# Last stage of a two-layer gated kernel: biases in a freed contraction row, transpositions between the halves of the up-projection, statistics and scaled products interleaved

## The chip, the cores and the metric

The kernel runs on one core of one Trainium2 chip, as one program from the first load to the last store. The metric is the device time of one execution in microseconds (us). The engines are PE (TensorE; PEld is its weight load), DVE (VectorE), ACT (ScalarE), POOL (GpSimd) and SP (SyncE, which issues the transfers).

## The reference, cut to what matters

Two layers work on x, 64 batches of 128 tokens by 256 values: cross attention and a routed feed-forward network, each scaled by tanh of a gate. Both networks get their input through a plain normalisation (mean taken off, divided by the root of the variance). The change touches the last network alone:

```python
# tail of reference(): xf is the normalised input, E = 4 experts, top 2
gate_scores = xf @ gate_W + gate_b
topk_scores, topk_idx = jax.lax.top_k(gate_scores, K_TOP)
weights = jax.nn.softmax(topk_scores, axis=-1)
def expert(w1, bb1, gg1, bbe1, w2, bb2, gg2, bbe2):
    h = jax.nn.relu(_layernorm(xf @ w1 + bb1, gg1, bbe1))
    return _layernorm(h @ w2 + bb2, gg2, bbe2)
...
exp_out = all_out[topk_idx, jnp.arange(BN)[:, None]]
out = jnp.sum(weights[..., None] * exp_out, axis=1)
return (out + xf).reshape(B, N, D)
```

The kernel adds tanh(gate) times this to its input x3. All four experts are computed for every token, and the weight of an unchosen one is zero.

## The kernel before, in words

There are four stages: attention of layer 0, the experts of layer 0, attention of layer 1, and the last stage, the feed-forward network of layer 1. The last stage goes through 64 batches b = 0..63 of 128 tokens, one step s for each, as a pipeline over several batches: in step s the up-projection works on batch s, the down-projection on s-1, the scaled products on s-2, the final sum on s-3. Steps 16 to 55 run in a loop of 8 steps a turn, the others are written out. Each engine has its own queue, which it works through strictly in the order in which `fstep` writes it; semaphores order the engines against each other. No planner or scheduler moves anything.

One batch goes this way (lines of the profile):

- DVE takes mean and variance of the input (`fst`, L1500, L1504), POOL makes the reciprocal root (`frs`, L645 to L651, four instructions), ACT writes the normalised `xf` (L824).
- PE transposes `xf` (L1151), ACT and DVE split it into a high and a low part (`xft_hi` L829, `xft_lo` L1490).
- PE: up-projection (L1117, L1120) in two halves of two experts each, into banks 2 and 3 of `ps`. Each half is one matmul for the bias (`ones2` by `b12`) and six for 2 blocks x (high.high, high.low, low.high), all 512 columns wide. The gate scores are six matmuls of 4 columns (L1142).
- DVE takes the statistics of the four experts (`h_st`, four instructions, then `h_mv`, four, L1423 and L1430), POOL makes scale and shift from them (`h_rs`, L670 to L676), ACT writes the normalised `z1` (L837, four), PE transposes it (L1184, eight), ACT applies scale, shift and relu (`a_t`, L857, eight).
- PE: down-projection (L1162 bias, L1165 eight matmuls, which the trace counts as sixteen) into banks 6 and 7. DVE takes statistics (`k_st`, `k_mv`), POOL makes `k_rs`, the weight times the reciprocal root `k_rw`, and mean times that (L631 to L638); DVE forms the scaled products `u2g` (L1454, four), POOL sums them (`u2s` L663, `u2t` L680), adds x3 (`rest` L682) and then the `mixed` part (L689).
- The weights of the chosen experts: DVE picks them (L1477 to L1486), ACT takes the exponential, DVE builds them (L1440 to L1447), POOL adds the two (L657), PE turns them (L1175), and one matmul adds shifts and means (L1130).

Three rules of the code matter below. `up1` of a batch waits until all four `z1` of the batch before are written (`z_act`). `u2g` waits until all four instructions of `k_rstd` are done. `h_rs` waits for all four `h_mv`.

Of the kernel before, what the change touches and what calls it, by code (L numbers as in the profile page):

```python
# [5 lines left out]
P = 128  # L6
# [118 lines left out]
def flamingo_gated(nc, x, ctx_in, consts, gates, wq, wk, wv, wp, b_proj, router, w1_0, b1_0, w2_0, b2_0,  # L125
                   gate_w, gate_b, w1_1, b12_1, g1_1, be1_1, w2_1, g2_1, be2_1, out):
# [25 lines left out]
    with es:  # L152
# [174 lines left out]
        gw_hi = psb("gw_hi", [P, C, E1], F32R)  # L327
        gw_lo = psb("gw_lo", [P, C, E1], F32R)
        gb_in = psb("gb_in", [P, E1])
        b12_in = psb("b12_in", [2, 2, E1, D])  # L330
        b12_hi = psb("b12_hi", [2, 2, E1, D], F32R)
        b12_lo = psb("b12_lo", [2, 2, E1, D])
        b12 = psb("b12", [P, 2, E1, D], F32R)
# [18 lines left out]
        def signals(prefix, arrivals, counts):  # L352
# [32 lines left out]
            dict(st=2, rstd=4, xf_done=1, x_turned=1, x_hi_done=1, x_lo_done=1, gates_done=1, gates_read=1, gate_steps=4,  # L385
# [31 lines left out]
        def _(sp):  # L417
# [20 lines left out]
            def layer1_weights():  # L438
                sp.wait_ge(s_padded, 3)
                for dst, src in ((w1f, w1_1), (w2f, w2_1), (gw_in, gate_w), (gb_in, gate_b), (b12_in, b12_1), (g1_in, g1_1),  # L440
                                 (be1_in, be1_1), (g2_in, g2_1), (be2_in, be2_1)):
                    sp.dma_start(dst[0:E1] if dst is be2_in else dst[:], src).then_inc(s_fw, 16)
                sp.dma_start(be2_in[E1:2 * E1], g2_1[0]).then_inc(s_fw, 16)
# [96 lines left out]
        def _(pool):  # L540
# [83 lines left out]
            def fstep(s):  # L624
# [14 lines left out]
                b = s + 1  # L639
                if b.within(B):  # L640
                    st = f["rstd"]
                    pool.wait_ge(f["st"].of(b), f["st"].at(b))
                    if (b - 1).begun:
                        pool.wait_ge(f["xf_done"].of(b - 1), f["xf_done"].at(b - 1))
                    nc.gpsimd.tensor_tensor(frs[:, 0:1], fmv[:, 1:2], eps, ALU.add).then_inc(st.sem, 1)  # L645
                    pool.wait_ge(st.of(b), st.at(b, 1))
                    nc.gpsimd.tensor_tensor(frs[:, 1:2], frs[:, 0:1], neg_half, ALU.pow).then_inc(st.sem, 1)
                    pool.wait_ge(st.of(b), st.at(b, 2))
                    nc.gpsimd.tensor_tensor(frs[:, 2:3], fmv[:, 0:1], frs[:, 1:2], ALU.mult).then_inc(st.sem, 1)
                    pool.wait_ge(st.of(b), st.at(b, 3))  # L650
                    nc.gpsimd.tensor_tensor(frs[:, 3:4], frs[:, 2:3], neg_one, ALU.mult).then_inc(st.sem, 1)  # L651
# [6 lines left out]
                b = s - 2  # L658
                if b.within(B):
                    pool.wait_ge(f["u_done"].of(b), f["u_done"].at(b))  # L660
                    if (b - 1).begun:
                        pool.wait_ge(f["summed"].of(b - 1), f["summed"].at(b - 1))
                    nc.gpsimd.tensor_tensor(u2s[:], u2g[:, 0:2, :], u2g[:, 2:4, :], ALU.add).then_inc(f["halved"].sem, 1)  # L663
# [14 lines left out]
                if b.within(B):  # L678
                    pool.wait_ge(f["halved"].of(b), f["halved"].at(b))
                    nc.gpsimd.tensor_tensor(u2t[:], u2s[:, 0, :], u2s[:, 1, :], ALU.add).then_inc(f["summed"].sem, 1)  # L680
                    pool.wait_ge(f["summed"].of(b), f["summed"].at(b, 1))
                    nc.gpsimd.tensor_tensor(rest[:, b.parity, :], u2t[:], x3[:, b.off % 8, :], ALU.add).then_inc(f["summed"].sem, 1)  # L682
                b = s - 3
                if b.within(B):
# [4 lines left out]
                    nc.gpsimd.tensor_tensor(x4[:, b.parity, :], rest[:, b.parity, :], mixed[:, b.parity, :], ALU.add).then_inc(f["mix"].sem, 1)  # L689

            pool.wait_ge(s_fset2, 10)
# [4 lines left out]
        def _(act):  # L696
# [113 lines left out]
            act.wait_ge(s_fw, 16 * 10)  # L810
            nc.scalar.activation(w1_hi[:], w1f[:], ACT.Copy).then_inc(s_fset, 1)
            nc.scalar.activation(gw_hi[:], gw_in[:], ACT.Copy).then_inc(s_fset, 1)
            nc.scalar.activation(b12_hi[:], b12_in[:], ACT.Copy).then_inc(s_fset, 1)
            nc.scalar.activation(be2_in[0:2 * E1], be2_in[0:2 * E1], ACT.Copy, scale=g_t[0:2 * E1, 3:4]).then_inc(s_fset, 1)
            act.wait_ge(s_fset, 4)
            act.wait_ge(s_fset2, 10)

            def fstep(s):
                b = s + 1
                if b.within(B):  # L820
                    act.wait_ge(f["rstd"].of(b), f["rstd"].at(b))
                    if (b - 8).begun:
                        act.wait_ge(f["mixed_done"].of(b - 8), f["mixed_done"].at(b - 8))
                    nc.scalar.activation(xf[:, b.off % 8, :], x3[:, b.off % 8, :], ACT.Identity, scale=frs[:, 1:2], bias=frs[:, 3:4])\  # L824
                        .then_inc(f["xf_done"].sem, 1)
                    act.wait_ge(f["x_turned"].of(b), f["x_turned"].at(b))
# [22 lines left out]
                b = s  # L849
                if b.within(B):  # L850
                    if (b - 2).begun:
                        act.wait_ge(f["down1_done"].of(b - 2), f["down1_done"].at(b - 2))
                    for e in range(E1):
                        if e % 2 == 0:
                            act.wait_ge(f["z_turned"].of(b), f["z_turned"].at(b, e // 2 + 1))
                        for c in range(C):
                            nc.scalar.activation(a_t[:, b.parity, e, c, :], ps[:, 4 + e // 2, (e % 2 * 2 + c) * P:(e % 2 * 2 + c + 1) * P],  # L857
                                                 ACT.Relu, scale=g1_in[:, e, c:c + 1], bias=be1_in[:, e, c:c + 1])\
                                .then_inc(f["a_done"].sem, 1)
# [5 lines left out]
        def _(pe):  # L865
# [240 lines left out]
            pe.wait_ge(s_fset2, 10)  # L1106

            def fstep(s):
                b = s
                if b.within(B):  # L1110
# [3 lines left out]
                    for half in range(2):  # L1114
                        dst = ps[:, 2 + half, :]
                        two = slice(2 * half, 2 * half + 2)
                        pe.matmul(dst, ones2[:], b12[:, 0, two, :].rearrange("p e n -> p (e n)"), start=True, stop=False)  # L1117
                        for c in range(C):
                            for xt, w in ((xft_hi, w1_hi), (xft_hi, w1_lo), (xft_lo, w1_hi)):
                                mm = pe.matmul(dst, xt[:, b.parity, c, :], w[:, c, two, :].rearrange("p e n -> p (e n)"),  # L1120
                                               start=False, stop=(c == C - 1 and xt is xft_lo))
                        mm.then_inc(f["up1_done"].sem, 1)
# [9 lines left out]
                if b.within(B):  # L1132
# [6 lines left out]
                    k = 0  # L1139
                    for c in range(C):  # L1140
                        for xt, w in ((xft_hi, gw_hi), (xft_hi, gw_lo), (xft_lo, gw_hi)):
                            mm = pe.matmul(ps[:, 1, 128:128 + E1], xt[:, b.parity, c, :], w[:, c, :], start=(k == 0), stop=(k == 5))  # L1142
                            k += 1
                    mm.then_inc(f["gates_done"].sem, 1)
                b = s + 1
                if b.within(B):
# [3 lines left out]
                    for c in range(C):  # L1150
                        mm = pe.transpose(ps[:, 0, c * P:(c + 1) * P], xf[:, b.off % 8, c * P:(c + 1) * P], ident)  # L1151
                    mm.then_inc(f["x_turned"].sem, 1)
                b = s - 1
                if b.within(B):
                    if (b - 1).begun:
                        pe.wait_ge(f["u_done"].of(b - 1), f["u_done"].at(b - 1))
                    for e in range(E1):
                        if e % 2 == 0:
                            pe.wait_ge(f["a_done"].of(b), f["a_done"].at(b, 4 * (e // 2) + 4))
                        dst = ps[:, 6 + e // 2, (e % 2) * D:(e % 2 + 1) * D]  # L1160
                        if e % 2 == 0:
                            pe.matmul(ps[:, 6 + e // 2, :], ones2[:], b12[:, 1, e:e + 2, :].rearrange("p e n -> p (e n)"),  # L1162
# [13 lines left out]
                b = s  # L1176
                if b.within(B):
                    if (b - 1).begun:
                        pe.wait_ge(f["a_done"].of(b - 1), f["a_done"].at(b - 1))
                    for e in range(E1):  # L1180
                        if e % 2 == 0:
                            pe.wait_ge(f["z_act"].of(b), f["z_act"].at(b, e + 2))
                        for c in range(C):
                            mm = pe.transpose(ps[:, 4 + e // 2, (e % 2 * 2 + c) * P:(e % 2 * 2 + c + 1) * P],  # L1184
                                              z1[:, b.parity, e, c * P:(c + 1) * P], ident)
                        if e % 2 == 1:
                            mm.then_inc(f["z_turned"].sem, 1)
# [5 lines left out]
        def _(dve):  # L1193
# [12 lines left out]
            for n in range(2):  # L1206
# [140 lines left out]
                if n == 0:  # L1347
# [43 lines left out]
                    nc.vector.memset(b12[:].bitcast(F32), 0.0).then_inc(s_padded, 1)  # L1391
# [4 lines left out]
            dve.wait_ge(s_fw, 16 * 10)  # L1396
# [4 lines left out]
            nc.vector.tensor_tensor(gw_lo[:], gw_in[:], gw_hi[:], ALU.subtract).then_inc(s_fset2, 1)  # L1401
            nc.vector.tensor_tensor(b12_lo[:], b12_in[:], b12_hi[:], ALU.subtract).then_inc(s_fset2, 1)
            dve.wait_ge(s_fset2, 5)

            nc.vector.tensor_scalar(b12_lo[:], b12_lo[:], hilo_mask[:, 1:2], None, ALU.mult).then_inc(s_fset2, 1)
            dve.wait_ge(s_fset2, 6)
            nc.vector.scalar_tensor_tensor(out=b12[0:2].rearrange("p a e n -> p (a e n)"),
# [182 lines left out]
```

## Time and profile before

| | us |
|---|---|
| median of 3 runs (lowest, highest) | 2548.15 (2542.39, 2556.09) |
| the profiled execution's own time | 2547.97 |
| its span in the trace | 2546.2 |
| last stage: first to last up-projection | 1878.38 to 2511.48 |
| PE busy over the span | 2336.5 (92%) |
| DVE, ACT, POOL busy over the span | 1640.8, 1155.4, 1131.4 |

The granted TensorE clock is 0.979 on average. Busy shares are averages over four unlike stages; the rows below are therefore of the last stage alone. A PE row's length is modelled, and matmuls overlap, so the distance from one start to the next is what counts on PE. POOL's lengths are rough as well.

### The profile page before, as it was taken

Reading aid. Unit: us, or ns where it says so; the run is one execution under the profiler, and the core shown is the slowest. Engines: PE = TensorE matmul, PEld = TensorE weight load, DVE = VectorE, ACT = ScalarE, POOL = GpSimd, SP = SyncE. Lnnn points to the kernel's source line nnn. Section 1 sums busy time; section 2 is a strip of 40 time slices with the busy share of each in tenths; the row PEclk is TensorE's granted clock in tenths of the full one; section 3 lists DMA queues with packets and bytes.
Section 4 is the critical chain, followed back from the end, with each engine's and each line's share of the span. In section 5 each row is a group of like instructions: output and inputs, shape, how many; then the busy total and the mean of one; then the engine's idle time right before and its main releaser. Section 6 shows DMA issues by size and latency. Waiting matters only on the chain.

```text
span 2546.2 us, 57620 instructions
## 1 busy us (share of the span) xinstructions
PE 2336.5 (92%) x19280; PEld 1934.2 (76%) x19280; DVE 1640.8 (64%) x4890; ACT 1155.4 (45%) x2327; POOL 1131.4 (44%) x2072
## 2 busy tenths in 40 slices
PE   6998989999699999999799999999969999999997
PEld 4777777777499998999666676676748887878885
DVE  4776767777455565555355555555557877777775
ACT  3444544454233333333244444444436565556563
POOL 3455555555200000000244444444327777777776
PEclk9999999999799999999899999999979999999998
DMA  8111111112221122221111111111200000000000
GB/s 266 46 56 54 56 52 54 56 56 72 96 85 56 64 86 86 71 84 50 58 55 58 58 57 58 54 56 58 76 23 28 26 29 27 25 25 29 25 25 16
DMA packets 125253, 147.10 MB, mean 58 GB/s; under 512 B 13818, under 2 KB 117506, under 8 KB 122754
## 3 DMA queue, kind: packets, MB, share of 16 engines
q1 hardware_dynamic: 118916, 127.80, 15.5%
q0 software_dynamic: 6144, 16.79, 2.1%
q8 instruction: 114, 1.87, 0.3%
q14 instruction: 79, 0.65, 0.1%
HBM read 85.82 MB, written 58.72 MB: 57 GB/s over the span
## 4 chain that ended last, share of the span: by engine, by line
PE 71%; DVE 11%; issue 8%; POOL 4%; ACT 4%; DMA 1%; SPq 1%; POOLq 0%; DVEq 0%; ACTq 0%
PE ps L1098 11%; PE ps L1083 10%; PE ps L924 7%; PE ps L1005 5%; PE ps L1165 5%; PE ps L954 5%; PE ps L885 4%; PE ps L1120 4%; PE ps L900 4%; PE ps L938 3%; PE ps L948 3%; DVE o_n L1233 2%; PE ps L989 2%; PE ps L880 2%; ACT z L837 2%
## 5 line engine op out<-in xcount | busy, mean ns | idle before, releaser
L1216 DVE TENSOR_REDUCE nmax<-ps 128x8 f32<-128x1024 f32 x256 | 311.7, 1223 | 102.6 <-PE ps L900 96.1
L553 POOL TENSOR_TENSOR km_r<-qk,cst 128x512 fp32r<-128x512 f32 x128 | 153.5, 1199 | 407.9 <-ACT qk L733 407.9
L801 ACT ACTIVATE hid<-ps,b_in 128x512 f32<-128x512 f32 x192 | 132.4, 690 | 371.7 <-PE ps L1083 371.7
L709 ACT ACTIVATE prob_t<-ps 128x1024 f32<-128x1024 f32 x256 | 248.1, 1021 | 95.3 <-PE ps L885 95.3
L578 POOL COPY slot_in<-slot_all 128x1 int32 (+1 forms) x64 | 11.4, 178 | 575.9 <-DMA eo_d<-eo 575.9
L1165 PE MATMUL ps<-w2f,a_t 128*128 128x256 f32 x1024 | 243.4, 381 | 0.0
L1098 PE MATMUL ps<-w_hi,hid_hi 128*128 128x256 f32 x768 | 219.1, 285 | 0.0
L1098 PE MATMUL ps<-w_hi,hid_lo 128*128 128x256 f32 x768 | 217.3, 283 | 0.0
L1098 PE MATMUL ps<-w_lo,hid_hi 128*128 128x256 f32 x768 | 217.3, 283 | 0.0
L1165 PEld LDWEIGHTS ps<-w2f,a_t 128*128 128x128 f32 x1024 | 195.5, 191 | 27.3
L733 ACT ACTIVATE qk<-ps 128x512 f32<-128x512 f32 x128 | 76.4, 597 | 282.8 <-PE ps L954 282.8
L837 ACT ACTIVATE z<-ps,h_rs 128x256 f32<-128x256 f32 x256 | 123.5, 563 | 152.5 <-POOL h_rs L676 152.5
L857 ACT ACTIVATE a_t<-ps,be_in,g_in 128x128 f32<-128x128 f32 x512 | 182.7, 447 | 0.8 <-PE ps L1184 0.2
L1222 DVE TENSOR_TENSOR nmax_x<-ps,cst 128x512 fp32r<-128x512 f32 x128 | 88.5, 692 | 140.7 <-PE ps L975 140.7
L1083 PE MATMUL ps<-xgt_hi,w_hi 128*128 128x512 f32 x384 | 150.5, 392 | 3.7 <-issue 2.2
L938 PE MATMUL ps<-w_v,c_t 128*128 128x256 f32 x512 | 148.4, 413 | 3.4 <-DMA c_t<-in_ctx_in_dram 3.4
L1083 PE MATMUL ps<-xgt_lo,w_hi 128*128 128x512 f32 x384 | 150.1, 391 | 0.0
L1083 PE MATMUL ps<-xgt_hi,w_lo 128*128 128x512 f32 x384 | 150.1, 391 | 0.0
L1454 DVE SCALAR_TENSOR_TENSOR u2g<-ps,k_rw,g_in 128x256 f32<-128x256 f32 x256 | 106.2, 478 | 67.8 <-POOL gw L638 67.8
L1386 DVE TENSOR_TENSOR eo<-ps,b_in 128x256 f32<-128x256 f32 x96 | 34.0, 418 | 177.8 <-PE ps L1098 177.8
L1098 PEld LDWEIGHTS ps<-w_lo,hid_hi 128*128 128x128 f32 x768 | 147.4, 192 | 0.0
L1098 PEld LDWEIGHTS ps<-w_hi,hid_hi 128*128 128x128 f32 x768 | 147.2, 192 | 0.0
(190 smaller groups left out, 6278.9 us busy)
## 6 DMA issues: line engine op xcount, KB each, us to landing
c_t<-in_ctx_in_dram SPq DMA_DIRECT2D x128, 128.0 KB, 2.0
x_d<-x SPq DMA_DIRECT2D x128, 128.0 KB
w_raw<-in_w_dram SPq DMA_DIRECT2D x16, 1024.0 KB, 7.7
slots_d<-zeros SPq DMA_DIRECT2D x12, 1024.0 KB, 8.7
xg<-slots_d SPq DMA_DIRECT2D x24, 512.0 KB, 4.7
eo_d<-eo SPq DMA_DIRECT2D x24, 512.0 KB, 3.2
x_in<-in_x_dram SPq DMA_DIRECT2D x64, 128.0 KB, 2.1
x_in<-x_d SPq DMA_DIRECT2D x64, 128.0 KB, 2.1
```

The costliest lines, as they stand in the source:

```text
L553: nc.gpsimd.tensor_tensor(dst, src.unsqueeze(2).to_broadcast([P, 2, 2, P]), head_mask.unsqueeze(1).unsqueeze(3).to_broadcast([P, 2, 2, P]) ...
L709: nc.scalar.activation(prob_t[:, 8 * h:8 * h + 8, :].rearrange("p a k -> p (a k)"), scores[:, 2 * h:2 * h + 2, :].rearrange("p a k -> p (a ...
L801: nc.scalar.activation(hid[:, fc % 2, :], ps[:, 4 + fc % 2, 0:G], ACT.Gelu, bias=b1_in[:, e.parity, fc:fc + 1]).then_inc(z["hid_done"].sem, 1)
L837: nc.scalar.activation(z1[:, b.parity, e, :], ps[:, 2 + e // 2, (e % 2) * D:(e % 2 + 1) * D], ACT.Identity, scale=h_rs[:, 1, e:e + 1], bia ...
L857: nc.scalar.activation(a_t[:, b.parity, e, c, :], ps[:, 4 + e // 2, (e % 2 * 2 + c) * P:(e % 2 * 2 + c + 1) * P], ACT.Relu, scale=g1_in[:, ...
L924: mm = pe.matmul(b5[32 * g:32 * g + 32, j * P:(j + 1) * P], v_aug[:, p, h, :], prob_t[:, r, :], start=True, stop=True, tile_position=(0, 3 ...
L938: mm = pe.matmul(b6[:, 0:D], c_t[:, b.off % 4, c, :], w_v[:, c, :], start=(c == 0), stop=(c == C - 1))
L954: mm = pe.matmul(b5[:, (part + m) * P:(part + m + 1) * P], w[:, c, m * P:(m + 1) * P], src[:, c, :], start=(c == 0), stop=(c == C - 1))
L1083: mm = pe.matmul(ps[:, 4 + fc % 2, 0:G], w[:, q, at:at + P], xt[:, g.parity, c, :], start=(k == 0), stop=(k == 5))
L1098: mm = pe.matmul(ps[:, i, 0:D], hd[:, fc, i * P:(i + 1) * P], w[:, q, at:at + D], start=(fc == 0 and k == 0), stop=(fc == FC - 1 and k == 2))
L1165: mm = pe.matmul(dst, a_t[:, b.parity, e, c, :], w2f[:, e, c, :], start=False, stop=True, skip_group_check=True)
L1216: nc.vector.tensor_reduce(nmax[:, b.parity, 2 * h:2 * h + 2, 0:4], scores[:, 2 * h:2 * h + 2, :].rearrange("p a (r k) -> p a r k", k=P), A ...
```

## The change

1. **Biases.** The normalised input sums to zero over its 256 values. So the first value is minus the sum of the others, its row of the weights can be subtracted from the other 255 rows, and the contraction row that is freed takes the constant 1 and the bias. `xf` gets a 257th column that holds 1, and PE transposes columns 1 to 256. The subtraction (`w1f - w1_first`, `gw_in - gw_first`) is done once on DVE ahead of the stage, from a further 1 MB load. The two bias matmuls of the up-projection and DVE's bias for the gate scores go; the bias of the down-projection stays.
2. **Gate scores.** Four matmuls in place of six: the high part of the input by high and low weights side by side (8 columns), the low part by the high weights (4 columns). DVE adds the two groups of 4 columns with two instructions in place of one.
3. **Order on PE:** first half of up(b), transpositions of z1(b-1), second half of up(b), then the rest as before.
4. **Order on DVE:** statistics of the first half of h(b), two scaled products, statistics of the second half, `h_mv`, the other two scaled products. Before: four scaled products, then the statistics of both halves.
5. **Order on POOL and ACT:** on POOL `h_rs` goes ahead of `u2s`, and `frs` to the end of the step, one batch further ahead. On ACT `a_t` goes one step later, to the place ahead of `xft_hi`.
6. The down-projection waits for two scaled products ahead of each half, where it waited for all four.

```diff
 # PE
+            def up(b, half):
+                two = slice(2 * half, 2 * half + 2)
+                for c in range(C):
+                    for xt, w in ((xft_hi, w1_hi), (xft_hi, w1_lo), (xft_lo, w1_hi)):
+                        mm = pe.matmul(ps[:, 2 + half, :], xt[:, b.parity, c, :], w[:, c, two, :].rearrange("p e n -> p (e n)"),
+                                       start=(c == 0 and w is w1_hi and xt is xft_hi), stop=(c == C - 1 and xt is xft_lo))
+                mm.then_inc(f["up1_done"].sem, 1)
...
-                        pe.matmul(dst, ones2[:], b12[:, 0, two, :].rearrange("p e n -> p (e n)"), start=True, stop=False)
...
+                    for c in range(C):
+                        pe.matmul(ps[:, 1, 128:128 + 2 * E1], xft_hi[:, b.parity, c, :], gw_hl[:, c].rearrange("p h e -> p (h e)"),
+                                  start=(c == 0), stop=False, skip_group_check=True)
+                        mm = pe.matmul(ps[:, 1, 128:128 + E1], xft_lo[:, b.parity, c, :], gw_hl[:, c, 0, :],
+                                       start=False, stop=(c == C - 1), skip_group_check=True)
...
+                            if (b - 1).begun:
+                                pe.wait_ge(f["u_done"].of(b - 1), f["u_done"].at(b - 1, e + 2))
...
 # DVE, ahead of the stage
-            dve.wait_ge(s_fw, 16 * 10)
+            dve.wait_ge(s_fw, 16 * 11)
+            nc.vector.tensor_tensor(w1f[:], w1f[:], w1_first[:], ALU.subtract).then_inc(s_fset2, 1)
+            nc.vector.tensor_tensor(gw_in[:], gw_in[:], gw_first[:], ALU.subtract).then_inc(s_fset2, 1)
...
 # DVE, in a step
+                b = s
+                if b.within(B):
+                    stats(2, h_st, f["h_stats"], f["up1_done"], b, 0)
                 b = s - 2
                 if b.within(B):
                     dve.wait_ge(f["k_rstd"].of(b), f["k_rstd"].at(b))
...
+                    scaled(b, 0)
                 b = s
                 if b.within(B):
-                    stats(2, h_st, f["h_stats"], f["up1_done"], b, 0)
                     stats(2, h_st, f["h_stats"], f["up1_done"], b, 1)
                     stats_in_all(h_st, h_mv, f["h_stats"], b)
+                b = s - 2
+                if b.within(B):
+                    scaled(b, 1)
+                b = s
+                if b.within(B):
                     dve.wait_ge(f["gates_done"].of(b), f["gates_done"].at(b))
-                    nc.vector.tensor_tensor(gpad[:, b.parity, 0:E1], ps[:, 1, 128:128 + E1], gb_in[:], ALU.add).then_inc(f["gates_read"].sem, 1)
+                    nc.vector.tensor_copy(gpart[:], ps[:, 1, 128 + E1:128 + 2 * E1]).then_inc(f["gates_half"].sem, 1)
+                    dve.wait_ge(f["gates_half"].of(b), f["gates_half"].at(b))
+                    nc.vector.tensor_tensor(gpad[:, b.parity, 0:E1], ps[:, 1, 128:128 + E1], gpart[:], ALU.add).then_inc(f["gates_read"].sem, 1)
```

How this stands on the engines, in one of the written-out steps at the end of the stage. First POOL before, from the first instruction of a step:

```order
L631 TENSOR_TENSOR k_rs<-k_mv,cst 128x4 [waits f_u_done,f_k_stats]
L633 TENSOR_TENSOR k_rs<-k_rs,cst 128x4 [waits f_k_rstd]
L636 TENSOR_TENSOR k_rw<-k_rs,gw 128x4 [waits f_k_rstd,f_gwt_done]
L638 TENSOR_TENSOR gw<-k_mv,k_rw 128x4 [waits f_k_rstd]
L645 TENSOR_TENSOR frs<-fmv,cst 128x1 [waits f_xf_done,f_st]
L647 TENSOR_TENSOR frs<-frs,cst 128x1 [waits f_rstd]
L649 TENSOR_TENSOR frs<-fmv,frs 128x1 [waits f_rstd]
L651 TENSOR_TENSOR frs<-frs,cst 128x1 [waits f_rstd]
L657 TENSOR_TENSOR gw<-gwa,gwb 128x4 [waits f_gw_turned,f_gate_mix]
L663 TENSOR_TENSOR u2s<-u2g 128x512 [waits f_summed,f_u_done]
L670 TENSOR_TENSOR h_rs<-h_mv,cst 128x4 [waits f_z_act,f_h_stats]
```

And POOL in the changed kernel, the same stretch (lines are those of the changed file):

```order
L632 TENSOR_TENSOR k_rs<-k_mv,cst 128x4 [waits f_u_done,f_k_stats]
L634 TENSOR_TENSOR k_rs<-k_rs,cst 128x4 [waits f_k_rstd]
L637 TENSOR_TENSOR k_rw<-k_rs,gw 128x4 [waits f_k_rstd,f_gwt_done]
L639 TENSOR_TENSOR gw<-k_mv,k_rw 128x4 [waits f_k_rstd]
L645 TENSOR_TENSOR gw<-gwa,gwb 128x4 [waits f_gw_turned,f_gate_mix]
L652 TENSOR_TENSOR h_rs<-h_mv,cst 128x4 [waits f_z_act,f_h_stats]
```

Between `k_rs` and `h_rs` stood six instructions of POOL's own; now there is one. `frs` (four instructions) and `u2s` now follow after `h_rs`.

DVE before, from the first scaled product of a step:

```order
L1454 SCALAR_TENSOR_TENSOR u2g<-ps,k_rw,g_in 128x256 [waits f_halved,f_k_rstd]
L1454 SCALAR_TENSOR_TENSOR u2g<-ps,k_rw,g_in 128x256 x3
L1423 BN_STATS h_st<-ps 128x6 [waits f_up1_done]
L1423 BN_STATS h_st<-ps 128x6
L1423 BN_STATS h_st<-ps 128x6 [waits f_up1_done]
L1423 BN_STATS h_st<-ps 128x6
L1430 BN_AGGR h_mv<-h_st 128x2 [waits f_h_stats]
```

DVE in the changed kernel:

```order
L1433 BN_STATS h_st<-ps 128x6 [waits f_up1_done]
L1433 BN_STATS h_st<-ps 128x6
L1444 SCALAR_TENSOR_TENSOR u2g<-ps,k_rw,g_in 128x256 [waits f_halved,f_k_rstd]
L1444 SCALAR_TENSOR_TENSOR u2g<-ps,k_rw,g_in 128x256
L1433 BN_STATS h_st<-ps 128x6 [waits f_up1_done]
L1433 BN_STATS h_st<-ps 128x6
L1440 BN_AGGR h_mv<-h_st 128x2 [waits f_h_stats]
L1440 BN_AGGR h_mv<-h_st 128x2 x3
L1444 SCALAR_TENSOR_TENSOR u2g<-ps,k_rw,g_in 128x256 x2
L1483 COPY gpart<-ps 128x4 [waits f_gates_done]
L1485 TENSOR_TENSOR gpad<-ps,gpart 128x4 [waits f_gates_half]
```

Two statistics moved ahead of the wait for `k_rstd`, two scaled products behind `h_mv`; two scaled products and two statistics still stand between that wait and `h_mv`.

## Rows read from the trace of the kernel before

**Rows 1.** Busy time by stretch: from, to, length; busy and count per engine; clock

```profile
1960.18:1979.89 19.71, 19.43 (x105) 16.25 (x104) 15.81 (x71) 11.91 (x33) 15.61 (x34) 1.00 0.10 28
1878.38:2511.48 633.10, 615.90 (x3188) 511.74 (x3188) 492.35 (x2382) 370.29 (x999) 482.19 (x1054) 0.99 0.08 25
```

**Rows 2.** The critical chain over two steps: start, length, engine, tile, line

```profile
1962.56 1.66 DVE u2g L1454 x4
1964.21 1.34 DVE h_st L1423 x4
...
1968.38 1.48 ACT z L837 x3
...
1969.90 0.66 PE ps L1184 x4
1970.56 0.24 PE ps L1117
1970.79 1.40 PE ps L1120 x6
...
1974.25 0.56 PE ps L1142 x6
...
1980.31 0.21 POOL k_rs L631
```

**Rows 3.** POOL in order of time over one step: start, length, instruction, idle before

```profile
1960.61 0.20 POOL L631 TENSOR_TENSOR k_rs<-k_mv,cst 128x4 f32<-128x4 f32 x1 [0.69 <-DVE k_mv L1430]
...
1962.32 0.20 POOL L638 TENSOR_TENSOR gw<-k_mv,k_rw 128x4 f32<-128x4 f32 x1
1962.47 0.19 POOL L645 TENSOR_TENSOR frs<-fmv,cst 128x1 f32<-128x1 f32 x1
...
1963.78 0.20 POOL L657 TENSOR_TENSOR gw<-gwa,gwb 128x4 f32<-128x4 f32 x1
1964.29 1.27 POOL L663 TENSOR_TENSOR u2s<-u2g 128x512 f32<-128x512 f32 x1 [0.31 <-DVE u2g L1454]
1966.04 0.20 POOL L670 TENSOR_TENSOR h_rs<-h_mv,cst 128x4 f32<-128x4 f32 x1 [0.48 <-DVE h_mv L1430]
...
1967.84 0.72 POOL L680 TENSOR_TENSOR u2t<-u2s 128x256 f32<-128x256 f32 x1
...
1969.32 0.73 POOL L689 TENSOR_TENSOR x<-rest,mixed 128x256 f32<-128x256 f32 x1
1970.18 0.20 POOL L631 TENSOR_TENSOR k_rs<-k_mv,cst 128x4 f32<-128x4 f32 x1
```

**Rows 4.** DVE in order of time in the same step

```profile
1964.13 1.42 DVE L1423 BATCH_NORM_STATS2 h_st<-ps 128x6 f32<-128x256 f32 x4
1965.58 0.38 DVE L1430 BATCH_NORM_AGGREGATE h_mv<-h_st 128x2 f32<-128x6 f32 x4
1965.88 0.14 DVE L1463 TENSOR_TENSOR gpad<-ps,gb_in 128x4 f32<-128x4 f32 x1
...
1968.93 0.76 DVE L1423 BATCH_NORM_STATS2 k_st<-ps 128x6 f32<-128x256 f32 x2 [0.32 <-PE ps L1165]
1969.72 0.38 DVE L1430 BATCH_NORM_AGGREGATE k_mv<-k_st 128x2 f32<-128x6 f32 x4
```

**Rows 5.** PE in order of time, the step that follows

```profile
1970.31 0.48 PE L1117 MATMUL ps<-b,ones 128*128 128x512 f32 x1
...
1978.97 1.17 PE L1184 MATMUL ps<-cst,z 128*128 128x128 f32 x8
1979.89 0.47 PE L1117 MATMUL ps<-b,ones 128*128 128x512 f32 x1
```

**Rows 6.** DVE in order of time, ahead of the last stage

```profile
1865.10 2.29 DVE L1400 TENSOR_TENSOR w_lo<-w1f,w_hi 128x2048 fp32r<-128x2048 f32 x1 [1.69 <-ACT be_in L814]
...
1871.00 2.34 DVE L1407 SCALAR_TENSOR_TENSOR b<-b_hi,cst,b_lo 2x2048 fp32r<-2x2048 f32 x1
```

**Rows 7.** Waits of DVE in the looped steps: us in total, times, longest

```profile
DVE gsum L1440 <- issue: 11.6, 4, 3.2
```

More of the change, by code:

```diff
@@ L823, in fstep @@
                         act.wait_ge(f["mixed_done"].of(b - 8), f["mixed_done"].at(b - 8))
-                    nc.scalar.activation(xf[:, b.off % 8, :], x3[:, b.off % 8, :], ACT.Identity, scale=frs[:, 1:2], bias=frs[:, 3:4])\
+                    nc.scalar.activation(xf[:, b.off % 8, 0:D], x3[:, b.off % 8, :], ACT.Identity, scale=frs[:, 1:2], bias=frs[:, 3:4])\
                         .then_inc(f["xf_done"].sem, 1)
+                b = s - 1
+                if b.within(B):
+                    if (b - 2).begun:
+                        act.wait_ge(f["down1_done"].of(b - 2), f["down1_done"].at(b - 2))
+                    for e in range(E1):
+                        if e % 2 == 0:
+                            act.wait_ge(f["z_turned"].of(b), f["z_turned"].at(b, e // 2 + 1))
+                        for c in range(C):
+                            nc.scalar.activation(a_t[:, b.parity, e, c, :], ps[:, 4 + e // 2, (e % 2 * 2 + c) * P:(e % 2 * 2 + c + 1) * P],
+                                                 ACT.Relu, scale=g1_in[:, e, c:c + 1], bias=be1_in[:, e, c:c + 1])\
+                                .then_inc(f["a_done"].sem, 1)
+                b = s + 1
+                if b.within(B):
                     act.wait_ge(f["x_turned"].of(b), f["x_turned"].at(b))
@@ L848, in fstep @@
                     nc.scalar.activation(gw8_t[0:2 * E1, b.parity, :], ps[0:2 * E1, 1, 0:P], ACT.Copy).then_inc(f["gw_t_done"].sem, 1)
[L849 to L859, printed above, removed]
             run_steps(act, B, 4, 4, 11, fstep, SPAN)
@@ L1113, in fstep @@
                         pe.wait_ge(f["z_act"].of(b - 1), f["z_act"].at(b - 1))
-                    for half in range(2):
-                        dst = ps[:, 2 + half, :]
-                        two = slice(2 * half, 2 * half + 2)
-                        pe.matmul(dst, ones2[:], b12[:, 0, two, :].rearrange("p e n -> p (e n)"), start=True, stop=False)
-                        for c in range(C):
[L1119 to L1122, printed above, removed]
+                    up(b, 0)
+                b = s - 1
+                if b.within(B):
+                    if (b - 1).begun:
+                        pe.wait_ge(f["a_done"].of(b - 1), f["a_done"].at(b - 1))
+                    for e in range(E1):
+                        if e % 2 == 0:
+                            pe.wait_ge(f["z_act"].of(b), f["z_act"].at(b, e + 2))
+                        for c in range(C):
+                            mm = pe.transpose(ps[:, 4 + e // 2, (e % 2 * 2 + c) * P:(e % 2 * 2 + c + 1) * P],
+                                              z1[:, b.parity, e, c * P:(c + 1) * P], ident)
+                        if e % 2 == 1:
+                            mm.then_inc(f["z_turned"].sem, 1)
+                b = s
+                if b.within(B):
+                    up(b, 1)
                 b = s - 3
@@ L1430, in stats_in_all, with scaled @@
                     nc.vector.bn_aggr(mv[:, e, :], st[:, e, :]).then_inc(sig.sem, 1)
+            def scaled(b, half):
+                for e in (2 * half, 2 * half + 1):
+                    nc.vector.scalar_tensor_tensor(out=u2g[:, e, :], in0=ps[:, 6 + half, (e % 2) * D:(e % 2 + 1) * D],
+                                                   scalar=k_rw[:, e:e + 1], in1=g2_in[:, e, :],
+                                                   op0=ALU.mult, op1=ALU.mult).then_inc(f["u_done"].sem, 1)
             def fstep(s):
```

139 lines of the change are left out of this document (64 added, 75 removed).

## The prediction

> **What bounds the kernel now.** The change lies in the last stage, so I read that stage alone, in four views. First the busy times by stretch: over two steps in the middle of the written-out part PE is busy 19.43 of 19.71 us, DVE 15.81, POOL 15.61, ACT 11.91 [rows 1]. It looks like a stage bound by PE. The 63 intervals from the first to the last up-projection take 633.1 us [rows 1]; 63 at 19.71 / 2 = 9.855 would be 620.9, so 12.2 us lie in the first steps and in the loop's jumps.
>
> Second, PE in order of time: a step without a wait takes 1979.89 - 1970.31 = 9.58 us [rows 5], so the other one of a pair takes 10.13. PE's own work is thus 0.28 below the mean, and something else sets the pair.
>
> Third, the critical chain, which says what: it leaves PE and goes POOL k_rs, DVE u2g, DVE h_st, POOL h_rs, ACT z, PE, and back to k_rs after two steps, from 1960.61 [rows 3] to 1980.31 [rows 2]. That is 19.70 us, the measured pair. The loop is: k_rs of batch s-2, four scaled products, four statistics of batch s behind them in DVE's queue, h_rs, z, the last transpositions, then PE's up and down work of the next step, whose statistics feed k_rs of batch s.
>
> Fourth, POOL in order of time [rows 3]. POOL works 15.61 of 19.71 us, but its instructions depend on each other, and each dependent one starts 0.08 behind the end of the one before (u2t 0.72 long, then `rest`, then x: 1.48 from u2t to x, which is 0.72 + 0.08 + 0.68). By starts, one step of POOL is: k_rs to gw (L638) 1.71, gw to h_rs 3.72, h_rs to u2t 1.80, u2t to x 1.48, x until POOL is free 0.68: 9.39. And every second time k_rs starts with no wait at all (1970.18, no bracket; the time before it waited 0.69) [rows 3]. POOL's queue has next to no slack, though its busy share is 79%.
>
> **The change part by part.**
>
> *PE.* Two bias matmuls go: 0.24 each by the chain (six others take 1.40) [rows 2], 0.47. Two of six gate matmuls go: 0.56 / 6 = 0.09 [rows 2], at most 0.11 each, 0.2; an 8-column one is not in the trace, and I bound it by the 4-column ones below and a full 0.23 above, and take the former, since 4 columns cost as much as loading the weights. PE's step falls from 9.58 to 8.9.
>
> *z.* up of the next batch waits for all of z. The loop through it now is: half an up 1.40, eight transpositions 0.92 (1978.97 to 1979.89 [rows 5]), half an up 1.40, 0.2 until DVE sees it, two statistics 0.79 (as k_st to k_mv [rows 4]), h_mv to h_rs 0.46 (1965.58 to 1966.04 [rows 3, 4]), h_rs to PE's next start 3.86 (1966.04 to 1969.90 [rows 2, 3]): 9.0 us. The old two-step loop falls to 19.70 less two scaled products 0.79, two statistics 0.66 and PE's saving: some 18, 9.0 a step. Both are below 9.855. By these alone the change would gain.
>
> *POOL and DVE together.* This is where I see the loss. POOL's queue is now k_rs(s-2), gw, h_rs(s), u2s, u2t, rest, x, frs. h_rs(s) waits for h_mv(s), which on DVE stands behind two scaled products that wait for k_rstd(s-2), just made by POOL. So POOL ends k_rstd, has one instruction of 0.20 to do, and waits while DVE does its part; all the rest of its queue comes after. Before, the same hole was filled: frs 1.31 (1962.47 to 1963.78) and u2s 1.27 stood in it, which left waits of 0.31 and 0.48 [rows 3]. One step of POOL's loop, by starts:
> - k_rs to gw (L638): 1.71.
> - gw to h_rs: 3.72 before, with four scaled products (1.57, 1962.56 to 1964.13 [rows 2, 4]) and four statistics (1.45, 1964.13 to 1965.58 [rows 4]). With two of each, 0.785 and 0.79: 3.72 - 3.02 + 1.58 = 2.28.
> - h_rs to u2s: 1.80, as to u2t now.
> - u2s to u2t: 1.27 + 0.08 = 1.35; u2t to x 1.48; x to frs 0.68; frs to k_rs 1.31.
>
> The sum is 10.61 us, 0.75 more than 9.855. The halving takes 1.44 off the gap, and 1.31 + 1.35 of POOL's own work that lay in the gap now lies outside. It is a loop of one step and nothing else can shorten it. Is anything later than this? From the start of h_rs: the last two scaled products end at 0.65, the second half of the down-projection at 2.7, k_mv is with POOL at 4.2 by PE and at about 4.7 by DVE's own queue, while POOL comes to k_rs at 6.6. z ends at 3.85, PE's next up begins there, and its 3.72 end before DVE needs it. So the others have 0.8 to 2 us to spare, PE will stand idle about 1.8 us in a step, and none of it adds.
>
> Unseen transitions: u2s straight to u2t and x straight to frs. Below, with no gap, 10.4. Above, with a wait like those of 0.31 that POOL shows behind DVE, 10.85. I take 10.61, since all its pieces are spacings in this very trace.
>
> The Trainium skill has two rules here. Perfetto Trace Analysis, section Identifying the Most-Contended Engine, says to find the engine with the highest occupancy and optimise it first; by that, PE would be it and its 0.68 us a step a gain, some 40 us; this is the first rival. The same page, section GPSIMD Instruction, says to time GpSimd by the spacing of starts and not by reported lengths. The trace agrees in that 79% busy goes with a queue without a wait.
>
> *DVE, small parts.* One more instruction on 4 values, 0.14 like gpad [rows 4] plus 0.08 to wait for it, behind h_mv, beside POOL's work: nothing as long as DVE has 1.9 to spare; if not, 0.2 a step.
>
> *ACT.* a_t moves behind xf of the next-but-one batch and needs frs, which is now POOL's last. frs ends 6.6 after h_rs begins, xf and the eight a_t take 0.6 and 2.8, and z of the next batch is due at 12.4: nothing.
>
> *Set-up.* The subtraction of w1_first is one more 2.29 (as w_lo) on DVE, and ACT's w_hi, which ran in the attention stage's last wait, must now follow it. Against that the three steps for the bias, 5.95 from the end of w_lo (1867.39) to the end of b (1873.34) [rows 6], work on half as many values: about 3 less. DVE waited 1.69 for ACT and would wait about as long. I take nothing, between -1 and +1.5. The further 1 MB comes among loads that are done some 40 us before their use: nothing. The memset of the bias tile halves, under a transfer: nothing.
>
> *Jumps.* DVE waits at each of four jumps of the loop for instructions, 11.6 us in all, longest 3.2 [rows 7]. It will again; DVE has 1.9 to spare there, then gate weights and two statistics behind it, so about 1 us comes through each time. Of the 12.2 us outside the even steps I keep 5, between 0 and 12.
>
> *Sum.* 63 x 10.61 + 5 = 673.4 against 633.1: +40.3. On the profiled execution's 2547.97 that is 2588; it is 0.2 below the median of the runs, so the same number holds for them.
>
> **Rivals.**
>
> *PE or z is the bound (faster).* If POOL's hole costs nothing, because k_rstd of a batch is done so early that the two scaled products never hold up the statistics, the 9.0 of the z loop decides: 63 x 9.0 + 5 = 572, 61 less, 2487; with the first steps and jumps as before, 2494. For it: PE's busy share. Against it: POOL is in order, k_rstd(s-2) can't come before frs and x of the step before, and u2g already starts right behind its last instruction (1962.32 + 0.20 to 1962.56 [rows 2, 3]); it decides only if POOL's own eight blocks took 1.6 less than by their starts. 8%.
>
> *No change.* POOL's spans are rough. If 0.75 of the two unseen transitions and of h_rs to u2s falls away, the new loop ends at 9.86: 2548 less the few microseconds at jumps, 2540 to 2555. For it: one of two pairs in the old trace had POOL wait 0.69. Against: that wait is in the old loop's slack, not in these spacings. 6%.
>
> *The change doesn't do what it says.* The rows of the two queues show that it does; I give this nothing of its own.
>
> *The clock falls (slower still).* PE stands at 1.8 of 10.61 us where it stood at 0.28 of 19.7, in two gaps of about 0.9 and 1.0. The granted clock was 1.00 in the pair and 0.99 over the stage [rows 1]. If in one step out of ten PE ran at 1.2 GHz instead of 2.4, its 8.9 would be 17.8, 7 longer: 6 x 7 = 42 more, 2630. It decides when such a step is longer than 10.61. 4%.
>
> **How the numbers follow.** Forecast 82%: 10.4 to 10.85 a step and -1 to +7 beside it make 2573 to 2608. A run can be told from no change at about 0.5%, 13 us. Faster by that: the first rival 8% and a little of the second, 9%. Within it: 6%. Slower: 82 + 4 - 1 = 85%. The range takes the forecast's own and some of the ground towards the second rival: 2562 to 2610.
>
> **What would show it.** The spacing of k_rs on POOL is 10.6 in the even steps, with no wait before k_rs and one of about 1.9 before h_rs <- DVE h_mv; the critical chain goes POOL, DVE u2g and h_st, POOL, and no longer through PE or ACT; PE is busy about 84% of the stage, with waits for u2g ahead of the first bias matmul of the down-projection and for z ahead of up. Wrong, if k_rs waits for k_mv, if h_rs finds h_mv ready, or if a step is near 9.

## The result, and the profile after

The changed kernel takes 2587.74 us (median of 6 runs, 2579.16 to 2592.18); the kernel before, in the same comparison, 2552.12 (6 runs, 2542.39 to 2561.47). The ratio is 1.0137, interval 1.0106 to 1.0169: 1.4% slower, and forecast was 2588. The profiled execution took 2588.68 us, its span is 2586.9.

Busy time by stretch, two steps of the written-out part and then the 63 intervals from the first up-projection to the last, with the columns of [rows 1]:

```profile
1960.00:1981.30 21.30, 18.49 (x96) 15.11 (x95) 16.25 (x74) 11.64 (x33) 15.61 (x35) 1.00 0.08 26
1879.91:2552.27 672.36, 579.53 (x2928) 472.45 (x2928) 505.11 (x2441) 363.81 (x998) 480.22 (x1052) 1.00 0.07 23
```

The 63 intervals grew from 633.10 to 672.36 us, 39.3 more. The span grew by 40.7: what lies ahead of the last stage's first up-projection is 1.5 longer (1879.91 against 1878.38), and what follows the start of its last one is as long as before (2586.9 - 2552.27 = 34.6 against 2546.2 - 2511.48 = 34.7). So the loss lies where the stage repeats its step. PE is busy 86% of it against 97% before; the granted clock is 1.00.

POOL in order of time over one step, with the columns of [rows 3]:

```profile
1964.69 0.20 POOL L632 TENSOR_TENSOR k_rs<-k_mv,cst 128x4 f32<-128x4 f32 x1
...
1966.41 0.20 POOL L639 TENSOR_TENSOR gw<-k_mv,k_rw 128x4 f32<-128x4 f32 x1
1966.56 0.20 POOL L645 TENSOR_TENSOR gw<-gwa,gwb 128x4 f32<-128x4 f32 x1
1968.68 0.20 POOL L652 TENSOR_TENSOR h_rs<-h_mv,cst 128x4 f32<-128x4 f32 x1 [1.92 <-DVE h_mv L1440]
...
1970.47 1.27 POOL L664 TENSOR_TENSOR u2s<-u2g 128x512 f32<-128x512 f32 x1
1971.83 0.72 POOL L668 TENSOR_TENSOR u2t<-u2s 128x256 f32<-128x256 f32 x1
...
1973.33 0.74 POOL L677 TENSOR_TENSOR x<-rest,mixed 128x256 f32<-128x256 f32 x1
1974.03 0.19 POOL L684 TENSOR_TENSOR frs<-fmv,cst 128x1 f32<-128x1 f32 x1
...
1975.34 0.20 POOL L632 TENSOR_TENSOR k_rs<-k_mv,cst 128x4 f32<-128x4 f32 x1
```

This is the old [rows 3] with the hole emptied. Before, the time between gw and h_rs held frs and u2s and two small waits, 0.31 and 0.48; now it holds one instruction of 0.20 and a wait of 1.92, and frs and u2s stand behind. From k_rs to k_rs it is 10.65 us, and k_rs starts with no wait. The critical chain says the same; start, length, engine, tile and line as in [rows 2]:

```profile
1966.41 0.21 POOL gw L639
1966.64 0.88 DVE u2g L1444 x2
1967.52 0.68 DVE h_st L1433 x2
...
1968.68 0.21 POOL h_rs L652
...
1977.06 0.21 POOL gw L639
```

It closes after one step, on POOL and DVE alone; the old one went through ACT and PE and closed after two [rows 2]. The waits of the stage (1915 to 2520 us; microseconds in total, times, longest) show who stands still for it:

```profile
ACT xf L826 <- POOL frs L690: 152.6, 56, 2.8
ACT z L852 <- POOL h_rs L658: 124.5, 57, 2.5
DVE u2g L1444 <- POOL gw L639: 117.5, 52, 2.4
POOL h_rs L652 <- DVE h_mv L1440: 112.7, 57, 2.0
...
PE ps L1116 <- ACT z L852: 40.0, 56, 0.8
...
DVE gsum L1456 <- issue: 11.2, 4, 2.8
```

Two engines wait for each other once per step: DVE for POOL's gw (2.2), then POOL for DVE's h_mv (1.9). PE and ACT only wait for what they hand on.

### The profile page after: what moved, and what is told of

It reads as the page before. It is cut to its first block, busy times and chain, and to the rows that moved or that the text cites. A ratio compares the mean times of both kernels' runs of the same rounds, so it can differ in the third digit from the quotient of the medians.

```text
span 2586.9 us, 57194 instructions
## 1 busy us (share of the span) xinstructions
PE 2301.3 (89%) x19024; PEld 1897.7 (73%) x19024; DVE 1653.5 (64%) x4957; ACT 1149.8 (44%) x2327; POOL 1132.0 (44%) x2072
## 4 chain that ended last, share of the span: by engine, by line
PE 59%; POOL 17%; DVE 10%; issue 9%; ACT 2%; DMA 1%; POOLq 1%; SPq 1%; DVEq 0%; ACTq 0%
PE ps L1102 11%; PE ps L1087 10%; PE ps L928 7%; PE ps L958 5%; PE ps L1009 4%; PE ps L889 4%; PE ps L904 4%; PE ps L942 4%; POOL u2s L664 3%; PE ps L952 3%; POOL h_rs L654 3%; POOL k_rs L634 2%; DVE o_n L1240 2%; PE ps L993 2%; PE ps L884 2%
## 5 line engine op out<-in xcount | busy, mean ns | idle before, releaser
L579 POOL COPY slot_in<-slot_all 128x1 int32 (+1 forms) x64 | 11.4, 179 | 577.8 <-DMA eo_d<-eo 577.7
L1116 PE MATMUL ps<-w_hi,xft_hi 128*128 128x512 f32 x256 | 113.2, 442 | 49.9 <-ACT z L852 48.9
```

## The experiments

The theory, called A in the expectations: the step is the length of POOL's in-order queue around the wait for h_mv; what stands inside that wait is free, what stands outside counts in full. The rivals: B, it is ACT's new order; C, it is PE's work or z; D, it is the changed arithmetic with its extra small steps. (In the expectation of the third kernel, D stands for another claim: that PE's own work bounds the old kernel.) The kernels are the changed kernel with one edit more, but for the third, which undoes all the orders at once, and for those that build on the filled hole, where the text says so. Each was timed against the kernel before, which took 2550.04, 2553.17 and 2550.47 us in the three sets.

**The hole filled.** POOL's u2t and `rest` go into the gap between gw and h_rs, a batch later:

```diff
+                b = s - 3          # ahead of h_rs(s)
+                if b.within(B):
+                    ... u2t <- u2s, rest <- u2t, x
                 b = s
                 if b.within(B):
                     ... h_rs
 ...
-                b = s - 2          # behind u2s(s - 2)
-                if b.within(B):
-                    ... u2t <- u2s, rest <- u2t, x
```

> The changed kernel with one move on POOL: u2t and rest of the batch before (s-3) go ahead of h_rs, into the stretch in which POOL waits 1.92 us for h_mv; x stays behind u2s. Theory A (the step is POOL's in-order loop through DVE's two scaled products and two statistics): 0.80 + 0.70 us leave the loop, 10.65 becomes 9.15 a step, the whole 63 x 1.5 = 94 less than the changed kernel, about 2494; the wait before h_rs falls to about 0.4. Rival B (ACT's late a_t and xf, behind frs at POOL's end, set the step): frs still comes last, so no change beyond 10 us, about 2588. Rival C (PE or z binds as soon as POOL is relieved): not under 9.0 a step, 2485.

Measured: 2505.27 us (4 runs, 2501.06 to 2507.97), ratio to the kernel before 0.9828, interval 0.9788 to 0.9867. Moving two instructions took 82 us off the changed kernel and turned its loss into a gain. POOL, in order of time:

```profile
1974.63 0.74 POOL L649 TENSOR_TENSOR u2t<-u2s 128x256 f32<-128x256 f32 x1
1975.45 0.73 POOL L651 TENSOR_TENSOR rest<-u2t,x 128x256 f32<-128x256 f32 x1
1976.73 0.20 POOL L658 TENSOR_TENSOR h_rs<-h_mv,cst 128x4 f32<-128x4 f32 x1 [0.55 <-DVE h_mv L1440]
```

The two stand in the hole and leave a wait of 0.55 where 1.92 was. The step is 9.13 us: 10.65 less the 1.50 that u2t and `rest` take by starts would be 9.15. The time is still 11 us above the expected 2494. On PE the four steps with a jump of the loop take 11.2 to 11.4 us here against 9.16 for their neighbours, where the changed kernel has 11.1 against 10.73: with less slack more of each jump comes through, some 7 us in all. The rest lies mostly in the first steps of the stage. The chain of this kernel is another one:

```profile
1969.94 1.47 ACT z L852 x3
...
1971.55 1.62 PE ps L1116 x6
1973.17 0.87 PE ps L1135 x8
1974.04 1.40 PE ps L1116 x6
...
1976.73 0.21 POOL h_rs L658
```

That is the z loop of the prediction, priced there at 9.0. With POOL's loop shortened to about the same length, z takes over.

**More of the same.** On the kernel with the filled hole, the x of batch s-4 goes into the hole too, behind those two:

```diff
+                b = s - 4          # ahead of h_rs(s), behind u2t and rest
+                    ... x4 <- rest, mixed
 ...
-                b = s - 3
-                    ... x4 <- rest, mixed
```

> e1 and x too: x of batch s-4 goes into the same stretch ahead of h_rs, behind u2t and rest of s-3. Theory A: POOL's own work, 10.65 - 1.92 = 8.7 a step, is then without a wait, but e1 already stands at 9.13 by another loop (half an up, eight transpositions, half an up, two statistics, h_mv, h_rs, z: its chain names these alone), so 9.13 stays and the time is that of e1 within 5 us, 2505. If POOL's loop were what held e1, it would fall to about 8.9 a step by PE, 15 less, 2490.

Measured: 2506.67 us (6 runs, 2491.11 to 2509.59), ratio 0.9807 (0.9778 to 0.9836), the step 9.16. Nothing more came of it. The critical chain is a third one, two steps long:

```profile
1960.59 0.19 POOL k_rs L632
...
1967.12 1.48 ACT z L852 x3
...
1977.54 0.20 POOL frs L684
...
1978.90 0.19 POOL k_rs L632
```

From k_rs to k_rs it is 18.31 us, 9.16 a step. It runs through POOL's filled queue to h_rs, through z and both halves of the up-projection on PE, through DVE's queue down to fmv, and back over frs. So POOL's work is still on the chain here, but no longer in a loop with DVE alone.

**The arithmetic alone.** The folded biases, with the orders of all engines as they were before the change (POOL's is shown; those of DVE, PE and ACT are put back in the same way):

```diff
                 ... k_rs, gw (L638)
+                b = s + 1
+                    ... frs
                 b = s - 1
                     ... gw <- gwa, gwb
+                b = s - 2
+                    ... u2s
                 b = s
                     ... h_rs
-                b = s - 2
-                    ... u2s
 ...
-                b = s + 2
-                    ... frs
```

> The arithmetic of the change alone (biases in the freed row, four gate matmuls, DVE's two instructions for the gate scores) with the order of all engines as before. Theory A: the old two-step chain of 19.70 us loses PE's two bias matmuls and two gate matmuls, 0.67 once in two steps: 19.03, 9.52 a step, 63 x 0.34 = 21 less than before, about 2530. Rival D (PE's own work bounds the old kernel): 0.67 every step, 42 less, about 2508.

Measured: 2531.10 us (6 runs, 2524.88 to 2542.51), ratio 0.9927 (0.9894 to 0.9960). The step is 9.56 us against 9.855. In the profiled run the last stage began some 10 us later than in the changed kernel's (1890.2 against 1879.9), which is no work of that stage; the ratio comes from the medians. So the arithmetic gains 0.30 a step, though PE is spared 0.67: rival D falls, as the list has it and as the expectation has it (2508), and the other changes of order cost 10.65 - 9.56 = 1.09 a step. Its waits from 1950 to 2035 us, nine steps, show the old, filled hole, with a wait of 0.5 in it:

```profile
POOL h_rs L671 <- DVE h_mv L1440: 4.3, 9, 0.5
```

**DVE's order alone undone.**

```diff
                     scaled(b, 0)
+                    scaled(b, 1)
                 b = s
                 if b.within(B):
+                    stats(2, h_st, f["h_stats"], f["up1_done"], b, 0)
                     stats(2, h_st, f["h_stats"], f["up1_done"], b, 1)
                     stats_in_all(h_st, h_mv, f["h_stats"], b)
-                b = s - 2
-                if b.within(B):
-                    scaled(b, 1)
```

(and the first statistics ahead of the scaled products go.)

> The changed kernel with DVE's old order: four scaled products, then four statistics, h_mv. Theory A: the stretch of POOL's loop from gw to h_rs is 3.72 again in place of 2.28, with nothing of POOL's in it: 10.65 + 1.44 = 12.1 a step, 91 more than the changed kernel, about 2678. Rival B (ACT's order): no change, about 2588.

Measured: 2675.10 us (4 runs, 2674.28 to 2684.72), ratio 1.0502 (1.0455 to 1.0548), the step 12.07. The prediction's own terms give it: with 3.72 from gw to h_rs in place of 2.28, 10.61 + 1.44 = 12.05. POOL's wait rose by the same amount, 1.9 to 3.4:

```profile
POOL h_rs L652 <- DVE h_mv L1440: 23.5, 7, 3.4
```

Interleaving the scaled products and the statistics is thus the part of the change that helps, 1.4 us a step with this queue of POOL. What costs, by theory A, is that u2s and frs left the hole.

**ACT's order alone undone.** a_t(s-1) stands ahead of xf(s+1) again:

```diff
-                b = s + 1          # first in the step
-                    ... xf
                 b = s - 1
                     ... a_t
+                b = s + 1
+                    ... xf
```

> The changed kernel with one move on ACT: a_t of batch s-1 ahead of xf of batch s+1, so that relu no longer waits for frs, POOL's last. Theory A: ACT is beside the loop, no change, 2588, while PE's waits for a_t (48 us in all) turn into longer waits for u2g or z. Rival B (the late a_t sets the step): the 48 us of PE's waits for it go, about 2540.

Measured: 2597.00 us (4 runs, 2591.43 to 2600.82), ratio 1.0189 (1.0147 to 1.0230); the step is 10.65 as in the changed kernel. From 1950 to 2035 us PE waited 5.0 us in all for u2g in the changed kernel; here that wait is gone, and one for xf stands in its place. The wait that bounds stayed:

```profile
POOL h_rs L652 <- DVE h_mv L1440: 15.3, 8, 1.9
...
PE ps L1170 <- ACT xf L837: 7.6, 8, 1.0
```

Rival B falls. Of the 9 us between the medians (the two intervals overlap), the last stage of the profiled runs holds 1.7; where the rest comes from stays open.

**A useless instruction inside the hole, and the same one outside.** The twin test of A. An addition of 128x256 values (junk <- g_in, about 0.73 us) once per step, ahead of h_rs:

```diff
+                if (s - 2).within(B):     # between gw and h_rs
+                    nc.gpsimd.tensor_tensor(junk[:], g2_in[:, 0, :], g2_in[:, 1, :], ALU.add)
```

> The changed kernel with one useless instruction more on POOL in every step (128x256, the shape of u2t, into a tile that nobody reads), put ahead of h_rs, where POOL waits 1.92. Theory A: it fits into the wait, which falls to 1.2, and the time stays at 2588. If POOL's sum of work set the step and not the loop through DVE, 0.68 to 0.73 more each step, 44, 2632.

Measured: 2586.76 us (3 runs, 2582.55 to 2593.03), ratio 1.0141 (1.0110 to 1.0172), the step 10.64: nothing. POOL in order of time:

```profile
1975.47 0.73 POOL L648 TENSOR_TENSOR junk<-g_in 128x256 f32<-128x256 f32 x1
1977.44 0.20 POOL L655 TENSOR_TENSOR h_rs<-h_mv,cst 128x4 f32<-128x4 f32 x1 [1.24 <-DVE h_mv L1443]
```

The same two lines behind x, ahead of frs:

```diff
+                if (s - 2).within(B):     # between x and frs
+                    nc.gpsimd.tensor_tensor(junk[:], g2_in[:, 0, :], g2_in[:, 1, :], ALU.add)
```

> The same useless instruction, put behind x and ahead of frs. Theory A: it lies on POOL's loop with its whole spacing, 0.70 x 62 = 43 more, 2631, with the wait before h_rs still 1.92. Rival (POOL is not on the loop): no change, 2588.

Measured: 2631.87 us (3 runs, 2623.88 to 2640.18), ratio 1.0315 (1.0280 to 1.0350), the step 11.32:

```profile
1967.92 0.73 POOL L680 TENSOR_TENSOR junk<-g_in 128x256 f32<-128x256 f32 x1
...
1973.95 0.20 POOL L653 TENSOR_TENSOR h_rs<-h_mv,cst 128x4 f32<-128x4 f32 x1 [1.92 <-DVE h_mv L1443]
```

One instruction, 0.73 us: at one place the wait shrinks from 1.92 to 1.24 and the time stays; at the other the wait stays 1.92 and each step is 0.68 longer, 62 x 0.68 = 42 against 45 measured between the two medians. This shows A more directly than the rest.

**PE loaded again, with POOL as the bound and without.** Two bias matmuls come back into the up-projection. They carry the down-projection's bias, which is not zero here, though the first expectation takes it to be; so both kernels compute something else than the reference, and only their times are used. First in the changed kernel:

```diff
             def up(b, half):
                 two = slice(2 * half, 2 * half + 2)
+                pe.matmul(ps[:, 2 + half, :], ones2[:], b2_hl[:, two, :].rearrange("p e n -> p (e n)"), start=True, stop=False)
```

> The changed kernel with two bias matmuls of 512 columns put back into up, one ahead of each half (they add a bias of the right shape, which is zero in this data): 0.46 more of PE's work in a step. Theory A: PE stands idle 1.8 of 10.65 and up ends 1.1 before DVE needs it, so nothing changes, 2588. Rival (PE's work counts as before): 0.46 x 63 = 29 more, 2617.

Measured: 2593.14 us (3 runs, 2588.53 to 2598.40), ratio 1.0169 (1.0133 to 1.0206), the step 10.62. From 1950 to 2035 us PE's busy time rose from 73.81 to 77.82, which is the 0.5 a step, and the step did not grow. The interval overlaps the changed kernel's. Then the same edit on the kernel with the filled hole:

> e1 with the same two bias matmuls put back into up. Theory A: the loop that stands at 9.13 in e1 goes through both halves of up, so 0.46 more lies on it each step: 9.6, 29 more than e1, about 2534. If POOL held e1: no change, 2505.

Measured: 2532.21 us (4 runs, 2530.19 to 2535.99), ratio 0.9934 (0.9910 to 0.9959), the step 9.60 against 9.13, 0.47 more. The chain has them on it:

```profile
1969.59 0.87 PE ps L1136 x8
1970.46 0.23 PE ps L1114
```

So 0.47 us of PE's work is worth nothing in one order and 27 us in the other. Rival C falls for the changed kernel and holds for the filled one.

**The z loop cut as well.** On the kernel with u2t, `rest` and x in the hole, the first half of the up-projection waits only for the two z that read its bank:

```diff
                     if (b - 1).begun:
-                        pe.wait_ge(f["z_act"].of(b - 1), f["z_act"].at(b - 1))
+                        pe.wait_ge(f["z_act"].of(b - 1), f["z_act"].at(b - 1, 2))
                     up(b, 0)
 ...
                 if b.within(B):
+                    if (b - 1).begun:
+                        pe.wait_ge(f["z_act"].of(b - 1), f["z_act"].at(b - 1))
                     up(b, 1)
```

> e2 and one wait of PE shortened: the first half of up(s) writes the bank that only the first two z of the batch before read, so it waits for two z, and the second half for all four. Theory A: two z, 0.96, leave the loop that stands at 9.13 in e1; POOL's 8.7 and PE's own 8.9 remain, so about 8.95 a step, 63 x 0.18 = 11 less than e1, about 2494. If PE's records hide a longer own step, there is no gain over e2.

Measured: 2494.12 us (5 runs, 2490.19 to 2499.50), ratio 0.9779 (0.9754 to 0.9804), the step 8.95: the fastest of all, 2.2% below the kernel before and 3.6% below the changed one. Busy time from 1950 to 2035 us, and two waits in that stretch:

```profile
1950.00:2035.00 85.00, 85.00 (x447) 71.55 (x446) 75.04 (x349) 54.54 (x151) 73.76 (x162) 1.00 0.10 31
```

```profile
DVE u2g L1446 <- POOL gw L639: 7.7, 10, 0.9
POOL frs L684 <- DVE fmv L1528: 3.3, 9, 0.5
```

PE is busy 85.00 of 85.00 us here. Yet the critical chain runs on DVE and POOL, with no piece on PE:

```profile
1973.66 0.19 DVE fmv L1528
...
1973.92 0.20 POOL frs L684
...
1976.96 0.21 POOL gw L639
...
1977.19 0.88 DVE u2g L1446 x2
```

POOL now waits for fmv at the end of DVE's step, and DVE at the start of its next for POOL's gw. PE's own work (8.9 by the prediction's count) and this loop (8.95) are too close for the run to say which of them holds the step.

## Why the prediction was right, by its steps

*The step of 10.61.* It held, and so did its parts. By starts the changed kernel has 1.72 from k_rs to gw (1.71 forecast), 2.27 from there to h_rs (2.28), 1.79 to u2s (1.80), 1.36 to u2t (1.35), 1.50 to x (1.48), 0.70 to frs (0.68) and 1.31 to k_rs (1.31): 10.65 against 10.61. Each block is off by at most 0.02. The two transitions that the old trace did not show, u2s straight to u2t and x straight to frs, cost what any neighbours on POOL cost; the upper bound of 10.85 was not needed.

*The gap from gw to h_rs, less 1.44.* Shown on its own by putting DVE's order back: 12.07.

*frs and u2s outside, plus 2.66.* Shown by the twin test for an instruction of 0.73 us, and by the filled hole for two others. That these very two cost 2.66 was not run alone. Nor was PE's new order (with the down-projection's shorter waits); neither is on the chain of the changed kernel.

*What else is later.* k_mv was forecast to be with POOL 1.9 us before k_rs starts. On DVE, in order of time:

```profile
1972.92 0.38 DVE L1440 BATCH_NORM_AGGREGATE k_mv<-k_st 128x2 f32<-128x6 f32 x4
```

It is there at 1973.4, with the same 0.46 to POOL as h_mv, and k_rs starts at 1975.34: 1.96 to spare. That is why ACT's order and the bias matmuls moved nothing.

*PE's idle time.* Forecast 1.8 a step, in two gaps of about 0.9 and 1.0. PE in order of time:

```profile
1972.63 0.47 PE L1116 MATMUL ps<-w_hi,xft_hi 128*128 128x512 f32 x1 [0.76 <-ACT z L852]
...
1976.92 0.25 PE L1159 MATMUL ps<-gw_hl,xft_hi 128*128 128x8 f32 x1
1977.03 0.25 PE L1161 MATMUL ps<-gw_hl,xft_lo 128*128 128x4 f32 x1
...
1978.22 0.50 PE L1181 MATMUL ps<-b_hl,ones 128*128 128x512 f32 x1 [0.64 <-DVE u2g L1444]
```

The gaps are 0.76 and 0.64, for z and for u2g as forecast, 1.4 in all (18.49 busy of 21.30). The 8-column matmul is followed by the next after 0.11, as the 4-column ones are, the end that was taken.

*Outside the even steps, 5.* This term was mis-sized: it came to 672.36 - 63 x 10.65 = 1.4. Four jumps were to give about 1 us each; their steps are 11.10, some 0.4 each, since DVE's waits for instructions (11.2 us in all, [rows 7] had 11.6) met 1.96 of slack. The 40 looped steps run at 10.73 where the written-out ones have 10.65, 3.2 in all that the prediction did not have. In the loop DVE executes a small instruction that the written-out steps lack (the code puts it in where the batch is not known when the program is written), and one stands inside h_mv, on the loop of POOL and DVE:

```profile
2204.05 0.06 DVE L1202 MEMSET dve_tick<- 1x1 f32 x1
```

gw to h_rs is 2.36 there (2202.21 to 2204.57) against 2.27. And the first four intervals of the stage, where not all of POOL's queue has work yet, take 39.5, 3.1 less than four even steps; before they took 42.4, 3.0 more. The 5 of the prediction has no part for such a gain.

*The sum.* Its 673.4 is 1.0 above the measured 672.36: the step mis-sized by 0.04 gives 2.5 too little, the term outside 3.6 too much. With the 1.5 that the last stage began later, the profiled execution was met within half a microsecond, 40.7 against 40.3, because these cancel. That the median of 2587.74 stands on the forecast 2588 is luck as well: the forecast starts from 2548, the kernel before has 2552.12 in this comparison, and between the medians lie 35.6 us, not 40.3. What was right is the loop and its length.

*Slips in the working that moved nothing.* k_rs at 1970.18 was read as starting without any wait. It starts 0.46 behind k_mv at 1969.72, as h_rs does behind h_mv, and 0.86 behind x, where 0.68 was taken for x: POOL had 0.18 of slack. The old two-step loop, by its own terms, falls to 17.6 and not to some 18. And 10.4 to 10.85 a step with -1 to +7 beside it make 2574 to 2610, where 2573 to 2608 stands.

*Set-up, nothing between -1 and +1.5.* From the last x add to the first `fst` it is 11.25 against 11.62 before, so the set-up lies within its bounds; the 1.5 us by which the stage began later come from ahead of it. DVE:

```profile
1864.43 2.28 DVE L1404 TENSOR_TENSOR w1f<-w1f,w_first 128x2048 f32<-128x2048 f32 x1
...
1873.57 1.27 DVE L1416 SCALAR_TENSOR_TENSOR b_hl<-b_hi,cst,b_lo 2x1024 fp32r<-2x1024 f32 x1
```

The subtraction costs its 2.28, the wait for ACT is 1.69 as before, and the last bias step takes 1.27 where b took 2.34 [rows 6].

*The rivals.* PE or z as the bound was refused for this order and was right for another: with the hole filled the z loop decides at 9.13 (priced 9.0) and 2505 us (priced 2487 to 2494). The Trainium skill, Perfetto Trace Analysis, section Identifying the Most-Contended Engine, has one optimise the engine with the highest occupancy first, and judges TensorE's headroom by its arithmetic rate and the busy share of its weight loads. In the changed kernel PE has 86% by matmuls and 70% by weight loads, DVE 75%; yet half a microsecond more of PE's matmuls per step changed the step by nothing. The clock did not fall: 1.00 over the stage.

## What to carry to other kernels

When two in-order queues hand work to each other, write down the period by starts around the loop, wait included, for the old and the new order. What an engine does inside its wait for the other is free as long as it fits, and what it does outside counts in full as long as no other loop is longer, so a change that shortens the wait must be checked for what it pushed out of it; here two instructions moved back in were worth 82 us of 2588. An engine's busy share tells none of this: the same 0.5 us of PE's work cost 27 us in one order and nothing that could be told in the other.

## What the runs showed of the hardware that was not expected

A matmul of 8 columns takes as long as one of 4 here, 0.11 us from start to start, so folding two gate matmuls into one halves their cost. And what a jump of the loop costs depends on the slack behind it: each time DVE waits up to 2.8 us for instructions, of which 0.4 reached the step in the changed kernel, with 1.96 us to spare, and some 2 with the hole filled.
